# The head of an attention and mixture-of-experts kernel in another order

## The reference

```python
q, k = layernorm(x) @ Wq.T, ctx @ Wq.T
x = x + softmax(causal(q @ k.T / sqrt(128))) @ k
y = layernorm(x)
gates = softmax(y @ gate_W); top 2, normed -> cw
out = y
for e in range(8):
    out = out + cw[:, e:e+1] * (relu(y @ W1[e] + b1[e]) @ W2[e] + b2[e])
x = x + out
```

## Time and profile before

| | |
|---|---|
| three runs, us | 130.54, 131.43, 131.76 |
| median, us | 131.43 |
| profiled execution, us | 131.36 |
| its span, us | 129.6 |
| mean granted TensorE clock | 0.998 of full speed |
| TensorE busy | 120.8 us, 93% |
| VectorE busy | 106.3 us, 82% |
| ScalarE busy | 93.8 us, 72% |
| GpSimd busy | 53.7 us, 41% |
| loads and stores | 5.54 MB, 14.9% of the DMA engines' span |

### The profile page before, as it was taken

The page is one execution under the profiler, slowest core; times in us unless marked ns, Lnnn a source line. Parts: engine busy times, 40 slices in busy tenths (PEclk is TensorE's granted clock), DMA queues, the critical chain, the costliest instruction groups (busy, mean ns, idle before and its releaser), DMA issues. The chain is left out here.

```text
span 129.6 us, 3281 instructions
## 1 busy us (share of the span) xinstructions
PE 120.8 (93%) x1175; PEld 91.3 (70%) x1175; DVE 106.3 (82%) x403; ACT 93.8 (72%) x191; POOL 53.7 (41%) x57
## 2 busy tenths in 40 slices
PE   6987788999998999999999999999999989999991
PEld 2674566776866779777877768778766767776690
DVE  0619998998999999978898999958998799766683
ACT  3257457899776974998579937994799567989830
POOL 7298047311074953311095660330377403345400
PEclk9999999999999999999999999999999999999999
DMA  3999910000000000200000000200000002000002
GB/s 82 306 280 326 291 42 3 5 0 0 5 0 0 0 5 3 81 0 5 0 0 0 5 0 3 86 0 0 0 8 3 0 5 81 0 3 5 0 0 81
DMA packets 9904, 5.54 MB, mean 43 GB/s; under 512 B 504, under 2 KB 9888, under 8 KB 9888
## 3 DMA queue, kind: packets, MB, share of 16 engines
q1 hardware_dynamic: 9744, 5.27, 14.3%
q10 hardware_dynamic: 144, 0.07, 0.3%
HBM read 4.28 MB, written 1.05 MB: 41 GB/s over the span
## 5 line engine op out<-in xcount | busy, mean ns | idle before, releaser
L689 POOL TENSOR_TENSOR h_lo<-h,h_hi 128x512 f16<-128x512 f32 x24 | 28.7, 1196 | 39.8 <-ACT h L570 39.6
L570 ACT ACTIVATE h<-psH,b1T 128x512 f32<-128x512 f32 x64 | 43.4, 690 | 1.1 <-PE psH L506 0.9
L569 ACT ACTIVATE h_hi<-psH,b1T 128x512 f16<-128x512 f32 x48 | 33.0, 688 | 11.8 <-PE psH L385 11.8
L863 DVE SCALAR_TENSOR_TENSOR acc<-psY,weight_y,acc 128x128 f32<-128x128 f32 x125 | 35.1, 342 | 1.4 <-PE psY L406 1.2
L381 PE MATMUL psH<-x_hi,w_hi 128*128 128x512 f16 x62 | 23.5, 379 | 0.8 <-ACT h L570 0.8
L847 DVE TENSOR_TENSOR h_lo<-h,h_hi 128x512 f16<-128x512 f32 x24 | 16.5, 689 | 9.3 <-ACT h L570 9.0
L382 PE MATMUL psH<-x_hi,w_lo 128*128 128x512 f16 x62 | 23.5, 379 | 0.0
L385 PE MATMUL psH<-x_lo,w_hi 128*128 128x512 f16 x62 | 23.5, 379 | 0.0
L406 PE MATMUL psY<-w_hi,h_hi 128*128 128x128 f16 x192 | 22.7, 219 | 0.0
L406 PE MATMUL psY<-w_lo,h_hi 128*128 128x128 f16 x192 | 22.7, 219 | 0.0
L406 PEld LDWEIGHTS psY<-w_hi,h_hi 128*128 128x128 f16 x192 | 15.3, 98 | 2.2
(11 more groups left out here) (187 smaller groups left out, 190.2 us busy)
## 6 DMA issues: line engine op xcount, KB each, us to landing
w_sb<-in_L_ffn_W_dram SPq DMA_DIRECT2D x8, 256.0 KB, 4.7
out_dram<-acc SPq DMA_DIRECT2D x3, 256.0 KB, 2.3
x_sb<-in_x_dram SPq DMA_DIRECT2D x2, 256.0 KB, 4.4
ctx_sb<-in_ctx_dram SPq DMA_DIRECT2D x2, 256.0 KB, 4.8
x_sb<-in_x_dram SPq DMA_DIRECT2D x1, 512.0 KB, 6.8
ctx_sb<-in_ctx_dram SPq DMA_DIRECT2D x1, 512.0 KB, 7.4
out_dram<-acc SPq DMA_DIRECT2D x2, 128.0 KB, 1.8
wq_sb<-in_L_xattn_Wq_dram ACTq DMA_DIRECT2D x1, 64.0 KB, 2.7
```

Source lines behind the costliest of these rows:

```text
L569: nc.scalar.activation(h_hi[:, C * (e % 2) + c, :], psH[c][:, :], ACT.Relu, bias=bias, scale=scale)
L570: nc.scalar.activation(h[:, C * (e % 2) + c, :], psH[c][:, :], ACT.Relu, bias=bias, scale=scale).then_inc(h_ready, 1)
L689: nc.gpsimd.tensor_tensor(h_lo[:, i, :], h[:, i, :], h_hi[:, i, :], ALU.subtract).then_inc(hlo0_ready, 1)
L863: last = nc.vector.scalar_tensor_tensor(out=o, in0=y, scalar=weight_y[:, g % 2, t, e:e + 1], in1=o, op0=ALU.mult, op1=ALU.add)
```

## The change

- VectorE: `small_parts` no longer stands ahead of the inverted sums. Its products of gate_W and of b2 with SW go to ScalarE (two copies behind `probs_out`, ahead of b1T); the two differences stay on VectorE as `small_lo_parts`, behind the second variance and ahead of the norms.
- The copy of b2 covers all 96 partitions of `b2_rows`. To that end `b2_rows` is set to zero by GpSimd (its second instruction) ahead of the loads of b2, for which SP waits on `rows_zero`; the later zeroing of `b2_cat` goes.
- VectorE: the statistics of group 1 (`row_stats`) move from behind the second variance to ahead of the inverted sums.
- VectorE: w2_lo of pair 0 moves from ahead of `x_lo` to behind it.
- TensorE turns ctx of group 1 ahead of x; ScalarE takes `ctx_out` ahead of `x_out`.
- ScalarE: both halves of `x_hi` move ahead of `values_out`.

```diff
 # SP
             sp.dma_start(b1_rows[:, :], b1.rearrange("e (c p) -> (e c) p", p=P)).then_inc(small_in, 16)
+            sp.wait_ge(rows_zero, 1)
             for q in range(3):
                 sp.dma_start(b2_rows[32 * q:32 * q + E, :], b2).then_inc(small_in, 16)
 # TensorE
+            pe.wait_ge(ctx_in[1], 16)
+            ctx_transposes(1, ALL, FIRST_BANKS)
             pe.wait_ge(x_in[1], 16)
             x_transposes(1, ALL, FIRST_BANKS)
-            pe.wait_ge(ctx_in[1], 16)
-            ctx_transposes(1, ALL, FIRST_BANKS)
             key_product(1, ALL, FIRST_BANKS)
             value_product(1, ALL, FIRST_BANKS)
 # ScalarE
+            act.wait_ge(small_in, 16 * 5)
+            copy(gate_hi[:, :], gate_sb[:, :], small_hi, scale=SW)
+            copy(b2_cat[:, :], b2_rows[:, :], small_hi, scale=SW)
             act.wait_ge(b1_ps, 1)
             nc.scalar.activation(b1T[:, 0, :], psY[0][:, 0:E * C], ACT.Copy, scale=SX * SW)
             copy(b1T[:, 1, :], psY[0][:, 0:E * C], b1_ready, scale=SH)
+            ctx_out(1, ALL, FIRST_BANKS)
             x_out(1, ALL, FIRST_BANKS)
-            ctx_out(1, ALL, FIRST_BANKS)
             keys_out(1, ALL, FIRST_BANKS)
+            for ts, banks in HALVES:
+                x_hi_part(0, ts, banks)
             values_out(1, ALL, FIRST_BANKS)
-            for ts, banks in HALVES:
-                x_hi_part(0, ts, banks)
 # GpSimd
             nc.gpsimd.memset(ident[:, :], 0.0).then_inc(const_zero, 1)
+            nc.gpsimd.memset(b2_rows[:, :], 0.0).then_inc(rows_zero, 1)
...
-            nc.gpsimd.memset(b2_cat[:, :], 0.0).then_inc(const_ready, 1)
-            pool.wait_ge(const_ready, 4)
+            pool.wait_ge(const_ready, 3)
 # VectorE
-            def small_parts():
-                dve.wait_ge(small_in, 16 * 5)
-                dve.wait_ge(const_ready, 4)
-                nc.vector.tensor_scalar(gate_hi[:, :], gate_sb[:, :], SW, None, ALU.mult)
-                rows = [slice(32 * q, 32 * q + E) for q in range(3)]
-                for r in rows:
-                    last = nc.vector.tensor_scalar(b2_cat[r, :], b2_rows[r, :], SW, None, ALU.mult)
-                last.then_inc(small_hi, 1)
-                dve.wait_ge(small_hi, 1)
+            def small_lo_parts():
+                dve.wait_ge(small_hi, 2)
+                dve.wait_ge(const_ready, 3)
                 nc.vector.scalar_tensor_tensor(out=gate_lo[:, :], in0=gate_sb[:, :], scalar=SW, in1=gate_hi[:, :],
                                                op0=ALU.mult, op1=ALU.subtract)
...
             w1_lo_part(0)
-            small_parts()
-            for ts, banks in HALVES:
-                invert_sums(0, ts, chain)
...
             dve.wait_ge(x_in[1], 16)
             for t in range(TG, 2 * TG):
                 last = row_stats(t)
             chain.mark(last)
             for ts, banks in HALVES:
+                invert_sums(0, ts, chain)
...
+            for ts, banks in HALVES:
+                second_variance(0, ts, chain)
+            small_lo_parts()
+            for ts, banks in HALVES:
                 second_norm(0, ts)
-            chain.wait()
             mean_and_var(TG, 2 * TG, chain)
+            for ts, banks in HALVES:
+                x_lo_part(0, ts, banks)
             w2_lo_part(0)
-            for ts, banks in HALVES:
-                x_lo_part(0, ts, banks)
             mask_and_max(1, ALL, FIRST_BANKS)
```

More of the change, by code:

```diff
@@ L182, in xattn_moe @@
         out_done = sem("out_done")
-        warm_zero = sem("warm_zero")
+        warm_zero, rows_zero = sem("warm_zero"), sem("rows_zero")
         const_zero, const_ready = sem("const_zero"), sem("const_ready")
@@ L629, in _ @@
             copy(b1T[:, 1, :], psY[0][:, 0:E * C], b1_ready, scale=SH)
+            ctx_out(1, ALL, FIRST_BANKS)
             x_out(1, ALL, FIRST_BANKS)
-            ctx_out(1, ALL, FIRST_BANKS)
             keys_out(1, ALL, FIRST_BANKS)
-            values_out(1, ALL, FIRST_BANKS)
             for ts, banks in HALVES:
                 x_hi_part(0, ts, banks)
+            values_out(1, ALL, FIRST_BANKS)
             act.wait_ge(b1_ready, 1)
@@ L957, in w2_lo_part @@
                                                op0=ALU.mult, op1=ALU.subtract).then_inc(w2lo_ready, 1)
-            def small_parts():
-                dve.wait_ge(small_in, 16 * 5)
-                dve.wait_ge(const_ready, 4)
-                nc.vector.tensor_scalar(gate_hi[:, :], gate_sb[:, :], SW, None, ALU.mult)
-                rows = [slice(32 * q, 32 * q + E) for q in range(3)]
-                for r in rows:
-                    last = nc.vector.tensor_scalar(b2_cat[r, :], b2_rows[r, :], SW, None, ALU.mult)
-                last.then_inc(small_hi, 1)
-                dve.wait_ge(small_hi, 1)
+            def small_lo_parts():
+                dve.wait_ge(small_hi, 2)
+                dve.wait_ge(const_ready, 3)
                 nc.vector.scalar_tensor_tensor(out=gate_lo[:, :], in0=gate_sb[:, :], scalar=SW, in1=gate_hi[:, :],
                                                op0=ALU.mult, op1=ALU.subtract)
-                nc.vector.scalar_tensor_tensor(out=b2_cat[rows[2], :], in0=b2_rows[rows[2], :], scalar=SW,
-                                               in1=b2_cat[rows[2], :], op0=ALU.mult,
+                third = slice(64, 64 + E)
+                nc.vector.scalar_tensor_tensor(out=b2_cat[third, :], in0=b2_rows[third, :], scalar=SW,
+                                               in1=b2_cat[third, :], op0=ALU.mult,
                                                op1=ALU.subtract).then_inc(small_lo, 1)
@@ L977, in _ @@
             w1_lo_part(0)
-            small_parts()
+            dve.wait_ge(x_in[1], 16)
+            for t in range(TG, 2 * TG):
+                last = row_stats(t)
+            chain.mark(last)
             for ts, banks in HALVES:
@@ L988, in _ @@
                 second_variance(0, ts, chain)
[L989 to L992, removed]
+            small_lo_parts()
             for ts, banks in HALVES:
                 second_norm(0, ts)
-            chain.wait()
             mean_and_var(TG, 2 * TG, chain)
-            w2_lo_part(0)
             for ts, banks in HALVES:
                 x_lo_part(0, ts, banks)
+            w2_lo_part(0)
             mask_and_max(1, ALL, FIRST_BANKS)
```

## The result

| | before | changed |
|---|---|---|
| median of four runs each, us | 131.14 (130.54 to 131.76) | 129.56 (129.26 to 130.45) |
| profiled execution, us | 131.36 | 129.60 |
| its span, us | 129.6 | 127.8 |

The ratio is 0.988, with a 95% interval of 0.984 to 0.993: 0.7 to 1.6% faster, at the centre 1.2%, or 1.5 us. The prediction had said 130.3, with a range of 129.7 to 131.1.

The account below looks back on a forecast made before the run. The body was bound by TensorE's own work, its start by VectorE's order in the head. 1.03 + 0.02 - 0.20 + 0.30 = 1.15 us took the profiled 131.36 to 130.21, the median to 130.3, range 129.7 to 131.1.

Parts of the forecast that it names:

- The path: Head: VectorE's order up to gate_top of group 0, then ScalarE's gate exponent, sets when the body starts and so the end.
- Residual: VectorE, head: residual's second half starts at about 13.60 instead of 14.63, ended by a wait for attention; gain 1.03 us.
- rival of held reciprocals: VectorE's reciprocals held to 13.24 by GpSimd's w2_hi; residual gains 0.6 instead of 1.03, end 130.7; chance 0.15.
- small_lo_parts and the powers: VectorE's 0.50 us of small_lo_parts hides in the wait for GpSimd's two powers of 0.70 each; costs nothing.
- rival of held small parts: VectorE's small_lo_parts held by GpSimd's powers, norms at about 17.4; gain 0.6 in all, 130.8; chance 0.12.
- Collision: Norm 0 on VectorE holds up GpSimd's second power, starting within 0.05 us of it; loss 0.20, bounds 0 to 0.52.
- Shorter power, x_lo first: With VectorE in x_lo instead of w2_lo, GpSimd's power of group 1 takes 1.01 instead of 1.31; gain 0.30 us.
- ScalarE's copies: Copies of gate_hi and b2 on ScalarE ahead of b1T, 0.4 to 0.8 us together, hidden in a 0.96 us idle gap.
- ctx ahead of x, x_hi ahead of values_out: TensorE and ScalarE orders: ctx_out some 0.5 us earlier, clearing TensorE for xf's transposes; values wanted only far on.
- G: Time by which VectorE's gate_top of group 0 comes earlier, passed on to the end; 1.15 us, bounds 0.83 to 1.35.
- no collision: Rival: GpSimd's second power reads its input before norm 0; gain 1.35, median 130.1; chance 0.3.

Follow-up runs that it names:

- e5: Changed kernel with x ahead of ctx and values_out ahead of x_hi again; gate exponent 9.88 us behind ScalarE's second copy of probs, untimed.
- e8: Changed kernel with w2_lo(0) between small_lo_parts and the norms; gate exponent 9.96 us behind ScalarE's second copy of probs, untimed.
- e1: Changed kernel again, unaltered, timed in five rounds; ratio 0.989 (0.986 to 0.993) against the kernel before, median 129.53 us.
- e2: Kernel before the change again, unaltered, timed against itself in five rounds; ratio 1.001 (0.999 to 1.003).
- e4: Changed kernel with w2_lo(0) back ahead of x_lo; ratio 0.994 (0.991 to 0.997) against the kernel before.
- e7: Changed kernel with values_out ahead of x_hi again; gate exponent 9.57 us behind ScalarE's second copy of probs, untimed.
- e10: Changed kernel with gate_top(0) ahead of w1_lo(1) on VectorE; ratio 0.987 (0.982 to 0.991) against the kernel before.
- e11: Changed kernel with gate_top(0) ahead of w1_lo(1) and 7 instead of 9 warm-up products; ratio 0.984 (0.980 to 0.988) against the kernel before, median 129.0 us.
- e12: Changed kernel with the statistics of group 1 behind small_lo_parts; gate exponent 10.11 us behind ScalarE's second copy of probs, untimed.
- e9: Changed kernel with 7 instead of 9 warm-up products on TensorE; ratio 0.987 (0.983 to 0.991) against the kernel before.

## Why the prediction was off

*The path.* Right. TensorE's gap moved with the gate exponent: it stands 39.47 - 23.29 = 16.18 behind it before, 16.17 in the changed kernel, and 16.15 to 16.17 in all others except the two with the gate first, where the exponent is no longer the last to come. The body's stretch is the same, and TensorE's and ScalarE's surplus went unused: first hidden product 8.01 behind the mark before, 6.45 after, 1.56 earlier (predicted 1.2 to 1.4).

*Residual.* Right in size and in the engine that ends the gain: its second half starts 2.22 behind the mark before and 1.20 after, 1.02 earlier (1.03). But the wait for attention is that of its first half ("0.28 <-PE psD", at 0.67 behind the mark), which I had put at 12.85, or 0.44, without a wait. The second half follows 0.53 behind the first, about its pitch before (0.52), and in e5, whose first half comes at 0.79 without a wait, at the same 0.53. That attention's second half is through by then as well (13.07) made the sum come out: the size was in part luck. The reciprocals ran at 12.10 under GpSimd's w_hi and took 0.21: the rival of held reciprocals did not occur.

*small_lo_parts and the powers.* Right: it took 0.17 and 0.28 inside the first power, the powers 1.41 together. The rival of held small parts did not occur either.

*Collision.* **This term failed: priced at 0.20, it measured 0.** Norm 0 starts at 15.97, the second power at 15.20 + 0.70 = 15.90, and takes 0.70. Behind the four norms VectorE's aggregates stand 5.25 behind the mark against 6.29 before, 1.04 earlier, where I had 1.05 without a collision and 0.85 with it. I had let a norm start beside the power and hold it for nearly one norm's time.

Why nothing was held is not shown. One reading is the order of arrival: the norm is released 0.07 behind the power's start, and by then the power was past the part in which it can be held. In its favour, the power of 19.50 ended 0.86 and that of 36.53 0.89 us behind the end of the instruction that held it, which leaves at most 0.15 of their 1.01, and w2_lo in e8 came 0.02 too late to hold one. The rival is that a norm, with one input of such a size, holds no power at all. In its favour, in the kernel before the four statistics, also with one input in SBUF, ran from 16.90 to 17.77, one of them when the second power started at 17.42, and that power took 0.70 all the same. By either reading the rows on hand spoke for less than 0.20; no run puts a norm in front of a power.

*Shorter power, x_lo first.* Nearly right in size: the power takes 1.01, and the mask is 1.30 earlier against 1.35 without collision. The missing 0.05 is VectorE's: x_lo's second half starts 6.30 behind the mark in place of 6.24 (18.65), and the mask stands behind w2_lo, no longer behind the power. Wrong in whom I credited: without the orders the same exchange is worth nothing (9.83 to 9.88).

*ScalarE's copies.* Hidden: 0.20 and 0.30, where 0.4 to 0.8 was the bound. *ctx ahead of x, x_hi ahead of values_out.* The sum has no term for them. Each alone is worth nothing to 0.04, together they are worth 0.31, and the 0.30 of the shorter power depends on them.

*Sum.* G was 1.15 and is 1.31; the case "no collision" (1.35, chance 0.3) is the one that came. That explains 0.16 of the 0.74 us between 130.3 and 129.56. Another 0.29 is the reference: the median before was 131.43 of three runs when I predicted, 131.14 with the fourth, 130.8 in 24 others. The rest, 0.29, is not resolved by four runs of each: the interval of the ratio, 1.0% in width, holds 1.31 us (0.990) as well, and in the longer timing of e1 the medians differ by 1.27 us. So the **range was drawn too tight at its lower end**: it allowed 0.4 us for the wandering of a median next to a best case of 130.1, taken from a spread of 1.2 us among three runs, although the reference itself came out of these three and had its own error to be added.

## What to carry to other kernels

Before you price a reordered head, find a mark ahead of all edits and count from it: here it removed a disturbance of 1.3 us, as large as the effect, and made single profiles of the changed kernel agree to 0.01 us. Then look for what differs behind the mark too: the two profiles of the kernel before lie 0.19 apart there, for the held w1_lo of the next section. Move work to where its engine would wait for another engine anyway, and test orders together as well as alone: two of them were worth nothing to 0.04 us singly and 0.31 us as a pair. Last, look at the final releaser again, since putting one ready instruction (w1_lo) behind the one that is waited for gave another 0.4 us in the trace.

## What the hardware showed that I had not expected

**How long GpSimd holds VectorE.** w1_lo of pair 0, with two inputs in SBUF, runs beside GpSimd's TENSOR_SCALAR over 128x512, which takes about 1.5 us. In e2 GpSimd was first by 0.06 us:

```profile
10.31 1.49 POOL L705 TENSOR_SCALAR w_hi<-w_sb 128x512 f16<-128x512 f32 x1
10.37 1.10 DVE L950 SCALAR_TENSOR_TENSOR w_lo<-w_sb,w_hi 128x512 f16<-128x512 f32 x1
```

and VectorE took 1.10 instead of 0.69. In e4 VectorE was first by 0.16, took 0.69, and GpSimd took 1.88:

```profile
10.35 0.69 DVE L954 SCALAR_TENSOR_TENSOR w_lo<-w_sb,w_hi 128x512 f16<-128x512 f32 x1
10.51 1.88 POOL L709 TENSOR_SCALAR w_hi<-w_sb 128x512 f16<-128x512 f32 x1
```

From there on it is a matter of distance: behind GpSimd's start by 0.06, 0.09, 0.31, 0.37 and 0.73 us (e2, e5, e7, e1, the changed kernel) VectorE took 1.10, 1.06, 0.85, 0.78 and 0.69. The excess over 0.69 and the distance add up to 0.46 to 0.47 us in the first four. In e10, at 0.06 again, VectorE took 1.09. GpSimd's instruction holds VectorE for its first 0.46 us, not for its 1.49. The other order looks alike: behind VectorE's start by 0.12, 0.15, 0.16 and 0.30 us (e11, e12, e4, e9) GpSimd took 1.92, 1.88, 1.88 and 1.74, so its excess over 1.49 and the distance add up to 0.54 or 0.55 of VectorE's 0.69.

The Trainium skill, "SBUF — State Buffer", section "Who interferes with whom", says that the order of issue decides who blocks, and these traces agree. That the first one keeps the shared ports for the whole instruction it says outright of VectorE's two-port modes; of two SBUF inputs it says only that they contend with a GpSimd instruction that reads SBUF, and the prediction put the two together. For this pair the measured hold by GpSimd is a third of the instruction. It is where e2's 0.20, e5's 0.12 and e10's 0.16 us between mark and residual come from (residual's second half at 2.42 behind the mark against 2.22, and at 1.32 and 1.36 against 1.20).

**TensorE's pace at the start.** TensorE's stream up to the transposes of x is the same in all kernels with nine products, and the granted clock reads 1.00 throughout; yet the pace, 0.43 us for a product of 512 columns and half of that later, changes at anything from below 4.6 to near 7 us. These are the first transposes of x in e7, after the change, and the first transposes of ctx in e5, still before it:

```profile
4.59 0.38 PE L291 MATMUL psH<-ident,x_sb 128*128 128x128 f32 x2
```

```profile
6.48 0.62 PE L291 MATMUL psH<-ident,ctx_sb 128*128 128x128 f32 x2
```

A column of granted clock that reads 1.00 does not tell that TensorE is at its full pace; the duration of one shape does (272 ns for a transpose of 128x128 at the one, 421 ns at the other). What sets the moment no run here shows.
